# The low part of the experts' first weights on GpSimd: one operation, or eight

## The reference

```python
scores = softmax(xf @ gate_w.T); gate_vals, idx = top_k(scores, 6)     # 64 experts
...                                                                    # up to 128 tokens for each expert: xe
h = silu(einsum('ecd,eid->eci', xe, w1)) * einsum('ecd,eid->eci', xe, w3)
ye = einsum('eci,edi->ecd', h, w2)                                     # inner width 352
routed = (ye of each token and choice * gate_vals).sum over the choices
z = (silu(xf @ sw1.T) * (xf @ sw3.T)) @ sw2.T                          # shared expert, inner width 704
out = layernorm(x + routed + z)
```

## Time and profile before

| | |
|---|---|
| median of 3 runs | 3792.45 us (3791.91 to 3804.15) |
| the profiled execution | 3801.43 us, span 3799.7 us |
| TensorE busy in the span | 3257.2 us (86%), mean granted clock 0.943 |
| VectorE, ScalarE, GpSimd busy | 2419.0 us (64%), 1987.3 us (52%), 1698.6 us (45%) |
| `experts`, 2330 to 3712 us | TensorE 1207.9, VectorE 553.2, ScalarE 548.7, GpSimd 658.7 us of 1382 |

### The profile page before, as it was taken

The page is one execution under the profiler, slowest core; times in us unless marked ns, Lnnn a source line. Parts: engine busy times, 40 slices in busy tenths (PEclk is TensorE's granted clock), DMA queues, the critical chain, the costliest instruction groups (busy, mean ns, idle before and its releaser), DMA issues. The chain is left out here.

```text
span 3799.7 us, 57819 instructions
## 1 busy us (share of the span) xinstructions
PE 3257.2 (86%) x17410; PEld 2607.7 (69%) x17410; DVE 2419.0 (64%) x3621; ACT 1987.3 (52%) x3450; POOL 1698.6 (45%) x2191
## 2 busy tenths in 40 slices
PE   8999977899999999999999961989999988999980
PEld 6888855677666766676667640777777777777760
DVE  6777756888888888888888821443443344344334
ACT  2222226777777777777777711434343443444434
POOL 0000000156666666666666673444454554455442
PEclk9999988999999999999999965999999999999995
DMA  7666674466566656665666523555556565555648
GB/s 250 224 221 221 227 233 105 127 162 161 149 156 162 157 152 157 162 155 149 161 162 156 150 70 110 166 165 159 161 159 177 173 178 162 159 163 158 186 119 359
DMA packets 338371, 644.52 MB, mean 170 GB/s; under 512 B 39056, under 2 KB 137936, under 8 KB 333536
## 3 DMA queue, kind: packets, MB, share of 16 engines
q1 hardware_dynamic: 300000, 574.51, 49.5%
q0 software_dynamic: 35840, 50.60, 7.5%
q10 hardware_dynamic: 2304, 16.78, 1.0%
HBM read 422.90 MB, written 219.09 MB: 169 GB/s over the span
## 5 line engine op out<-in xcount | busy, mean ns | idle before, releaser
L746 DVE TENSOR_REDUCE att_neg_max<-att_ps_s 128x1 f32<-128x1024 f32 x512 | 606.5, 1217 | 80.9 <-PE att_ps_s L538 75.8
L651 ACT ACTIVATE att_prob<-att_ps_s,att_neg_max 128x1024 f32<-128x1024 f32 x512 | 570.7, 1116 | 120.7 <-DVE att_neg_max L746 103.7
L1034 POOL TENSOR_TENSOR exp_w_lo<-exp_w_raw,exp_w_hi 128x2816 fp32r<-128x2816 f32 x63 | 409.5, 6500 | 243.3 <-ACT exp_w_hi L1025 243.3
L538 PE MATMUL att_ps_s<-att_k,att_q 64*128 64x512 f32 x3072 | 434.0, 414 | 58.0 <-ACT att_prob L651 27.3
L834 POOL DMA_INDIRECT slots<-att_entry,att_slot x384 | 402.5, 1048 | 154.8 <-issue 98.7
L538 PEld LDWEIGHTS att_ps_s<-att_k,att_q 64*128 64x128 f32 x3072 | 279.8, 188 | 170.8 <-issue 128.0
L498 PE MATMUL att_ps_t<-att_ident,att_diff 128*128 128x128 f32 x2048 | 274.1, 277 | 80.5 <-ACT att_diff_lo L597 80.5
L693 DVE SCALAR_TENSOR_TENSOR att_diff<-att_prob,att_weight 128x1024 f32<-128x1024 f32 x256 | 328.5, 1283 | 7.1
L498 PEld LDWEIGHTS att_ps_t<-att_ident,att_diff 128*128 128x128 f32 x2048 | 225.2, 141 | 123.8 <-issue 116.1
L76 PE MATMUL exp_ps_ab<-exp_x_t,exp_sw_hi 128*128 128x512 f32 x704 | 284.4, 404 | 24.9 <-DVE exp_sw_lo L1326 24.9
L78 PE MATMUL exp_ps_ab<-exp_x_t,exp_sw_lo 128*128 128x512 f32 x704 | 276.4, 393 | 0.0
(11 more groups left out here) (210 smaller groups left out, 8582.3 us busy)
## 6 DMA issues: line engine op xcount, KB each, us to landing
exp_w_raw<-in_w_t SPq DMA_DIRECT2D x64, 1408.0 KB, 6.2
att_k<-k_parts SPq DMA_DIRECT2D x260, 256.0 KB
att_v<-v_parts SPq DMA_DIRECT2D x64, 1024.0 KB, 9.9
att_q<-q_parts SPq DMA_DIRECT2D x260, 128.0 KB
v_parts<-proj_v_out SPq DMA_DIRECT2D x64, 512.0 KB, 3.4
x_parts<-att_x_t SPq DMA_DIRECT2D x64, 512.0 KB
exp_x_t<-x_parts SPq DMA_DIRECT2D x16, 2048.0 KB, 12.7
exp_w_raw<-in_w_t SPq DMA_DIRECT2D x64, 512.0 KB, 4.8
```

The lines of the kernel that those rows point to most:

```text
L538: last = nc.tensor.matmul(ps_s[s][:, cols], q_buf[q % 2][rows, q_part, q_cols], k_buf[q % 2][rows, k_part, cols], start=m == 0, stop=m == 2)
L651: nc.scalar.activation(prob[s][i][:], ps_s[s][:], ACT.Exp, bias=neg_max[:, s, i : i + 1], accum_out=total).then_inc(exp_done[s], 1)
L746: nc.vector.tensor_reduce(neg_max[:, s, i : i + 1], ps_s[s][:], AX.X, ALU.max, negate=True).then_inc(max_done[s], 1)
L1034: engine.tensor_tensor(w13[1][:], w13_raw[:], w13[0][:].bitcast(F32), ALU.subtract).then_inc(w13_lo_done, 1)
```

## The change

`w13_low` makes eight subtractions of 128 x 352 in place of one of 128 x 2816: one for each of the four row tiles k, and in each for the columns of w1 and of w3. Only the last signals `w13_lo_done`. Nothing else is changed. The function serves GpSimd for 63 experts and VectorE for the first.

```diff
         def w13_low(eng, engine, e):
             eng.wait_ge(w13_hi_done, e + 1)
-            engine.tensor_tensor(w13[1][:], w13_raw[:], w13[0][:].bitcast(F32), ALU.subtract).then_inc(w13_lo_done, 1)
+            for k in range(KD):
+                for cols in (slice(0, INTER), slice(INTER, 2 * INTER)):
+                    last = engine.tensor_tensor(w13[1][:, k, cols], w13_raw[:, k, cols], w13[0][:, k, cols].bitcast(F32), ALU.subtract)
+            last.then_inc(w13_lo_done, 1)
```

## The result

The changed kernel takes 3828.04 us (median of 4 runs, 3826.67 to 3828.99), the kernel before 3793.68 us in the runs beside it. The ratio is 1.0085, with a 95% interval of 1.0066 to 1.0103: 34 us slower. The forecast was 3746 us, and the range, 3700 to 3800 us, missed it. It came out as rival B, which had 3824 us and a chance of 0.16.

A forecast was written before the change was run, and what follows sets the result against it. TensorE in the experts stage was held bound by its matmuls plus two waits and the clock. Costs of 6.3 us replacing 9.26 a group gain 44.5 us over 15, with the first group 46.5: 3746 us, range 3700 to 3800.

The forecast's parts named there:

- rival B: Experts stage: GpSimd never lets go of the port, VectorE waits for all eight pieces; +2.1 us a group, 3824 us, chance 0.16.
- The path: Experts stage: TensorE's waits for two low parts, plus the slow clock, cost 9.26 us a group above its matmuls.
- (a): GpSimd's low part of the weights: eight pieces cost more than one operation, +1.05 us taken.
- its other estimate, +0.3: GpSimd's pieces: the Trainium skill's rate, with 50 cycles a call, would make eight cost only about +0.3 us more.
- (b): First expert's turn: VectorE's hid subtraction waits for the first piece only; of the 6.3 us ps_y wait some 1.4 is left.
- (c): Last expert's turn, GpSimd on the path: longer low part, VectorE cutting in, later load; ps_a wait grows from 1.42 to 4.4 us.
- VectorE cutting into the pieces of turn 3: Last expert's turn: VectorE's w2 subtractions take the port before the eighth piece, delaying the low part 1.55 us.
- the 0.4 us for the later load: SP's later 1.4 MB weight load shares DMA engines with the scatter GpSimd awaits; 0 to 1.05 us, 0.4 taken.
- (d): TensorE's clock: the longer ps_a wait loses 1.56 us in every group; the ps_y wait shrinks to about 0.3, its clock loss gone.
- (e): First expert's low part in a group stays hidden behind TensorE's work, covered by 1.7 us where it had 10.8.

The follow-up runs named there:

- lining up: Changed kernel plus a one-column GpSimd memset and a wait for it ahead of the pieces in turns 0 and 3; 3735.23 us.
- the long memset: Changed kernel plus one-column memset, wait, then a 1024-column memset with the pieces queued behind it, in turns 0 and 3; 3761.54 us.

## Why the prediction was wrong

**The path (right).** The two waits, their order and their sum with the clock, 9.26 us a group, held. The fastest run with the z tiles moved gives nearly all of it back: 124 us of 15 x 9.26 = 139.

**(a) The price of the pieces (right).** 0.90 us apart and 7.25 us for eight, +0.97 us (it took +1.05; its other estimate, +0.3, is not borne out). Paid in full in turns 0 and 3: 13 to 18 us each, the clock included.

**(b) VectorE gets in: the step that failed.** It was carried over from L816 and L817. In these rows there are 0.08 us between the end of L816 and the start of L817 (1316.63, 1316.71), and no descriptors ahead of them. Nothing overlaps there, and without overlap VectorE does get in: in turn 1 of the changed kernel, after lining up, and behind the long memset. But the pieces that mattered stand right behind descriptors, where they overlap by 0.55 us, and VectorE stayed out for all eight: 80.1 us of waits for ps_y, where 5 were forecast. The prediction also let GpSimd's work, and its hold on the port, begin where the descriptors end (3049.29), though its own reading of the group had L1190 shut out from 3048.36. A sign of it was on record: L1034 has 6.26 us where it follows a wait and 6.8 and 6.7 us behind descriptors, 0.55 and 0.4 us longer, and the prediction named the port lost to a later record only as a point for rival B.

The page that the prediction set aside fits. The Trainium skill (GPSIMD Engine Reference, Instruction dispatch) says that the Q7 cores start the next instruction each for itself; the trace agrees behind descriptors, with its 0.55 us, and next to nothing of it shows elsewhere, with 0.04 us. The Trainium skill also says that a pair of the cores makes the descriptors (GPSIMD Engine Reference, When to use GPSIMD), and that a record starts with core 0 and ends with the last core (Perfetto Trace Analysis, GPSIMD Engine Instruction). That this pair falls behind the others is the inference on which S rests; no run here shows single cores. The runs show the overlap, that a wait for a one-column memset removes it, and that with it goes VectorE's being shut out.

**(c) The cost in turn 3 (right once in step).** With both turns lined up, the case that the forecast described, the waits for ps_a are 3.9 us a group (4.4 forecast), the longest subtraction of hid is 1.51 us (1.6), and the time is 3735 us (3746), lining up included, which has a price of its own, 0.2 to 0.3 us a turn. VectorE cutting into the pieces of turn 3 was taken at 1.55 us a group; by the waits for ps_a it is (58.6 - 39.1)/15 = 1.3 us, by the times of the two runs 1.5 to 1.8 us, with what lining up turn 3 costs by itself. Of the 0.4 us for the later load little is left: 38.1/15 = 2.54 us in the changed kernel is 1.42, 0.97 and about 0.15. In the changed kernel the term of 1.55 us is absent, since VectorE is shut out.

**(d) The clock (right for ps_a).** After 2.49 us of waiting the clock is at 0.50, and ps_a loses 1.56 us, in all 15 groups. That the loss ahead of ps_y would go hung on (b), and it stayed. **(e) The cover (no failure seen):** no wait for the first expert's low part. But the low part that ends later in turn 0 pushes the next turn's into VectorE's way, as the run with one operation in turns 1 to 3 showed, and the prediction had no term for that.

**Rival B** had the mechanism (the port is never free), and nearly the sum: +2.1 us a group, 3824 us, against 2.3 and 3828. It was wrong in that it held the back-to-back queue itself to be the cause: the runs with lining up have the same queue, and there VectorE gets in.

## What to carry to other kernels

Cutting a long GpSimd operation so that VectorE can share the port works only where the pieces hardly overlap: read their records. Where a piece outlasted its distance to the next by 0.06 us or less, VectorE got in; by half a us, never; by 0.1 us, now and then. Behind descriptors, try a one-column memset and a wait for it ahead of the work, or move the descriptors elsewhere; where GpSimd itself is what TensorE waits for, leave it out and keep one operation. A rival's evidence from tiny operations elsewhere in the program has to match in what stands ahead of them, not only in being queued.

## What was not expected of the hardware

A GpSimd operation behind descriptors takes the port before its record starts: VectorE's subtraction, recorded 0.40 us ahead of it, lost. So did all that came 0.48 us ahead or less, and none of those that came 0.49 us ahead or more; with lining up 0.02 us were enough. A wait for a memset of one column, which lets the operation end 0.2 to 0.3 us later, made the kernel with one operation 115 us faster (3678.0 us, ratio 0.9696). And an overlap of 0.1 us between pieces shut VectorE out for three pieces in one group, and let it in at the next change of pieces in another.
